# Causal attention inside a macaron block: score matmuls on 64-row tiles, and the maximum stream in two slots of two PSUM banks

## The reference

```python
q, k, v: (4, 1024, 16 heads, 16)
scores = einsum('bqhe,bkhe->bhqk', q, k) / sqrt(16)      # causal
attn = softmax(where(causal, scores, -inf), axis=-1)
out = einsum('bhqk,bkhe->bqhe', attn, v)
```

## Time and profile before

| | |
|---|---|
| three runs | 1534.96, 1540.11, 1540.85 us, median 1540.11 |
| profiled execution, its own time | 1542.46 us |
| its span, first to last instruction | 1540.8 us |
| TensorE busy, VectorE busy | 86%, 66% of the span |
| mean granted TensorE clock | 0.901 |
| softmax stage | about 502 to 1101 us |
| its maximum stream alone | 521.1 to 554.7 us |
| groups 0 to 14 with A units beside | 554.7 to 1067.8 us |

### The profile page before, as it was taken

How to read it: one execution, slowest core, us unless ns; L and a number is a source line. 1 busy time by engine, 2 the same in 40 slices (tenths; PEclk the granted TensorE clock), 3 DMA queues, 4 the chain that set the end, 5 groups by cost and what they waited for, 6 DMA issues and landing times. The chain is left out here.

```text
span 1540.8 us, 31184 instructions
## 1 busy us (share of the span) xinstructions
PE 1325.7 (86%) x8678; PEld 1003.7 (65%) x8709; DVE 1019.6 (66%) x2335; ACT 775.6 (50%) x1949; POOL 496.9 (32%) x651
## 2 busy tenths in 40 slices
PE   2628999899699499999998999999778269998998
PEld 1417999799588255555555555554465159997998
DVE  6594555499866777767675777773286755554787
ACT  2524556333244046666675666666546236564333
POOL 1554444255300201222211112212324554443454
PEclk9658999899899569999998999999896569999999
DMA  6503434122465712223322222200315114433233
GB/s 188 169 3 97 123 123 122 60 73 74 146 233 231 136 30 43 44 43 66 61 44 44 43 43 43 44 2 1 114 35 167 55 59 124 123 123 93 83 112 106
DMA packets 86509, 135.73 MB, mean 88 GB/s; under 512 B 12992, under 2 KB 66176, under 8 KB 83328
## 3 DMA queue, kind: packets, MB, share of 16 engines
q1 hardware_dynamic: 64896, 90.29, 22.1%
q0 software_dynamic: 13056, 35.67, 8.3%
q10 hardware_dynamic: 8448, 8.39, 1.6%
HBM read 81.35 MB, written 52.43 MB: 87 GB/s over the span
## 5 line engine op out<-in xcount | busy, mean ns | idle before, releaser
L1448 DVE TENSOR_REDUCE s_MX<-s_ps_a 128x1 f32<-128x512 f32 (+4 forms) x624 | 368.9, 643 | 133.8 <-PE s_ps_a L1515 132.2
L1422 ACT ACTIVATE s_PR<-s_ps_b 128x512 f32<-128x512 f32 (+3 forms) x768 | 343.7, 491 | 162.3 <-PE s_ps_b L1537 155.2
L1515 PE MATMUL s_ps_a<-s_KO,s_QO 96*128 96x512 f32 (+3 forms) x768 | 286.1, 422 | 22.7 <-DMA s_QO<-qk_scratch 22.7
L1537 PE MATMUL s_ps_b<-s_QO,s_KO 98*128 98x512 f32 (+3 forms) x768 | 266.6, 368 | 7.2 <-issue 3.9
L1391 POOL TENSOR_SCALAR_AFFINE_SELECT s_PR<-s_PR 128x256 f32<-128x256 f32 x256 | 103.5, 407 | 474.5 <-ACT s_PR L1422 473.6
L1537 PEld LDWEIGHTS s_ps_b<-s_QO,s_KO 98*128 98x128 f32 x768 | 146.3, 194 | 72.6 <-ACT s_PR L1422 54.4
L603 POOL DMA_INDIRECT f_XG<-xn_scratch,f_tok_u x144 | 136.4, 947 | 167.3 <-PE f_ps_x L700 157.4
L1515 PEld LDWEIGHTS s_ps_a<-s_KO,s_QO 96*128 96x128 f32 x768 | 152.1, 211 | 28.7 <-DVE s_MX L1448 20.8
L810 POOL DMA_INDIRECT f_YG<-y_scratch,f_slots_u x128 | 121.0, 945 | 150.2 <-DVE X L885 94.6
L1552 PE MATMUL s_ps_o<-s_PR,s_VG 128*17 128x512 f32 (+3 forms) x1536 | 163.0, 496 | 5.3 <-POOL s_PR L1391 5.3
L656 DVE TENSOR_TENSOR f_xl<-f_ps_x,f_xh 128x256 fp32r<-128x256 f32 x144 | 61.1, 425 | 97.7 <-ACT f_xh L628 92.6
(11 more groups left out here) (206 smaller groups left out, 2966.9 us busy)
## 6 DMA issues: line engine op xcount, KB each, us to landing
y_scratch<-f_YS SPq DMA_DIRECT2D x144, 128.0 KB
s_KO<-qk_scratch SPq DMA_DIRECT2D x48, 256.0 KB, 5.8
s_QO<-qk_scratch SPq DMA_DIRECT2D x96, 128.0 KB, 6.6
xn_scratch<-f_XN ACTq DMA_DIRECT2D x16, 512.0 KB, 3.2
qk_scratch<-p_QKh SPq DMA_DIRECT2D x32, 256.0 KB
qk_scratch<-p_QKl SPq DMA_DIRECT2D x32, 256.0 KB
f_stage<-in_w_up SPq DMA_DIRECT2D x20, 352.0 KB
X<-in_x SPq DMA_DIRECT2D x4, 1024.0 KB, 9.4
```

The costliest lines, as they stand in the source:

```text
L1422: nc.scalar.activation(PR[:, u // 2 % SLOTS, u % 2, 0:W - lo], ps_b[u % RING][:, lo:W], ACT.Exp, scale=SCALE).then_inc(exp_done, 1)
L1448: nc.vector.tensor_reduce(MX[:, h:h + heads, i, s], ps_a[v % RING][:, 0:heads * keys].rearrange("p (h n) -> p h n", h=heads), AX.X, ALU.ma ...
L1515: last = nc.tensor.matmul(ps_a[v % RING][:, at:at + keys], QO[k][0:R, h, i * P:(i + 1) * P], KO[k][0:R, h % 2, s * W:s * W + keys], start= ...
L1537: nc.tensor.matmul(ps_b[u % RING][:, lo:W], KO[k][0:RM, h % 2, i * P:(i + 1) * P], QO[k][0:RM, h, hf * W + lo:(hf + 1) * W], start=True, s ...
```

## The change

- **Operands.** The two heads of a pair go to rows 0 to 47 and 64 to 111 (48 rows a head: three parts of 16), the two max rows behind them at 48, 49 and 112, 113. Nothing is zero padded: QO is half as long, its memsets are gone, and VectorE sets rows 32 to 63 and 96 to 127 of every KO to one. A load is 12 DMAs of 128 KB (before: nine) with the same bytes, a `place_max` 4 DMAs of 8 KB (before: two of 16 KB).
- **Matmuls.** A and B matmuls have 48 and 50 rows and lie in rows 0 to 63 or 64 to 127 of the array. The two heads of a pair write to different banks.
- **A units.** A unit is both heads c of a pair in the two banks of a slot, up to 512 columns in each, read by one reduce of up to 1024 columns. A group has 21 units (before: 39). ps_a is two slots of two banks; ps_t is gone.
- **Masks.** With 64 rows the mask takes two matmuls (j = 0, 1) in each bank: four a diagonal unit, before one.
- **Turned tiles** use the slots of ps_a too, in one sequence with the A units (`USES`). Every use waits for the last reader of the use before the last (`slot_read`).
- **Order.** A unit counts by step are 3, 2, 1, 1, 2, 2, 2, 3, 2, 2, 1, 0 for steps 0 to 11 (in columns of VectorE 2560, 1536, 512, 1024, 1792, 1792, 2048, 2560, 1536, 2048, 1024, 0). `turn_output` and `turn_max` stand behind h = 1, ahead of the PV; on VectorE `normalise` and `max_low` stand behind the first A unit of the step and ahead of the others.

```diff
-    PH = 2 * HD
-    R = 3 * PH
+    R = 3 * HD
     RM = R + 2
+    TILE = P // 2
-            wide = W // keys
-            starts = range(0, GH, wide)
-            A_UNITS += [(i, s, h, min(wide, GH - h), keys) for h in starts]
+            wide = min(W // keys, 2)
+            A_UNITS += [(i, s, hp, wide, keys) for hp in range(0, 2, wide)]
...
+    OUT_T = MAX_T - 1
+    USES = []
+    for n in range(NB):
+        beside = [("a",) + one for one in A_BESIDE[n]]
+        USES += beside[:1]
+        if n == 1:
+            USES.append(("out", -1, 1))
+        if n == OUT_T:
+            USES.append(("out", 0, 0))
+        if n == MAX_T:
+            USES.append(("max", 1, 0))
+        USES += beside[1:]
...
-        ps_a = [ps(f"ps_a{i}", [P, W]) for i in range(RING)]
+        ps_a = [ps(f"ps_a{i}", [P, 2, W]) for i in range(2)]
-        ps_t = ps("ps_t", [P, W])
...
-            nc.vector.memset(QO[0][0:RM, :, :].bitcast(F32), 0.0).then_inc(zeros[0], 1)
-            nc.vector.memset(KO[0][R:RM, :, :].bitcast(F32), 1.0).then_inc(ones, 1)
+            for k in range(4):
+                for c in range(2):
+                    rows = slice(c * TILE + 32, (c + 1) * TILE)
+                    nc.vector.memset(KO[k][rows, :, :].bitcast(F32), 1.0).then_inc(ones, 1)
...
-                    nc.vector.tensor_reduce(MX[:, h:h + heads, i, s],
-                                            ps_a[v % RING][:, 0:heads * keys].rearrange("p (h n) -> p h n", h=heads),
-                                            AX.X, ALU.max).then_inc(a_read, 1)
+                    for c in range(2):
+                        dve.wait_ge(a_done[c], NA * g + v + 1)
+                    _, slot = slot_of_a(g, v)
+                    scores = ps_a[slot][:, :, 0:heads * keys].rearrange("p c (h n) -> p c h n", h=heads)
+                    nc.vector.tensor_reduce(MX[:, :, hp:hp + heads, i, s], scores, AX.X,
+                                            ALU.max).then_inc(slot_read, 1)
...
-                    if v >= RING or since(g, 1):
-                        pe.wait_ge(a_read, NA * g + v + 1 - RING)
+                    if not isinstance(g, int) or q >= 2:
+                        pe.wait_ge(slot_read, q - 1)
                     if diagonal:
-                        nc.tensor.matmul(scores[:, :, keys - P:keys], identb[:, :], neg[:, 0:heads, :],
-                                         start=True, stop=False, skip_group_check=True)
+                        for j in range(2):
+                            for c in range(2):
+                                rows = slice(c * TILE, (c + 1) * TILE)
+                                scores = banks[c][:, 0:heads * keys].rearrange("p (h n) -> p h n", h=heads)
+                                nc.tensor.matmul(scores[:, :, keys - P + j * TILE:keys], identb[rows, j, :],
+                                                 neg[rows, 0:heads, 0:P - j * TILE],
+                                                 start=j == 0, stop=False, skip_group_check=True)
+                    for hp in range(hp0, hp0 + heads):
+                        at = (hp - hp0) * keys
+                        for c in range(2):
+                            rows = slice(c * TILE, c * TILE + R)
+                            last = nc.tensor.matmul(banks[c][:, at:at + keys], QO[k][rows, hp, i * P:(i + 1) * P],
+                                                    KO[k][rows, hp, s * W:s * W + keys], start=not diagonal,
+                                                    stop=True, skip_group_check=True)
+                            if hp == hp0 + heads - 1:
+                                last.then_inc(a_done[c], 1)
...
-                nc.tensor.matmul(ps_b[u % RING][:, lo:W], KO[k][0:RM, h % 2, i * P:(i + 1) * P],
-                                 QO[k][0:RM, h, hf * W + lo:(hf + 1) * W], start=True, stop=True).then_inc(b_done, 1)
+                rows = slice(h % 2 * TILE, h % 2 * TILE + RM)
+                nc.tensor.matmul(ps_b[u % RING][:, lo:W], KO[k][rows, h // 2, i * P:(i + 1) * P],
+                                 QO[k][rows, h // 2, hf * W + lo:(hf + 1) * W],
+                                 start=True, stop=True).then_inc(b_done[h % 2], 1)
...
-                        if h == GH - 1:
-                            if n >= 1:
-                                pv_step(g, k, n - 1)
+                        if h == 1:
                             if n == 1 and since(g, 1):
                                 turn_output(g - 1, 1)
-                            if n == MAX_T - 1:
+                            if n == OUT_T:
                                 turn_output(g, 0)
                             if n == MAX_T and until(g, 1, NG):
                                 turn_max(g + 1)
+                        if h == GH - 1 and n >= 1:
+                            pv_step(g, k, n - 1)
```

More of the change, by code:

```diff
@@ L1258, in softmax_stage, with slot_use, slot_of_a @@
     MAX_T = 1 + max(n for n in range(NB) if (1, NA - 1) in A_BESIDE[n])
+    OUT_T = MAX_T - 1
[10 more added lines that the diff above has]
+        USES += beside[1:]
+    NU = len(USES)
+    FIRST = NA + 1 + AHEAD
+    def slot_use(g, what, ahead, index=0):
+        at = USES.index((what, ahead, index))
+        if not isinstance(g, int):
+            return FIRST - 1 + NU * g + at, (FIRST - 1 + at) % 2
+        q = FIRST + sum(0 <= n + use[1] < NG for n in range(g + 1) for use in USES[:at if n == g else NU])
+        return q, q % 2
+    def slot_of_a(g, v):
+        if isinstance(g, int) and g * NA + v < NA + AHEAD:
+            q = v + g * (NA + 1)
+            return q, q % 2
+        ahead = 1 if v >= AHEAD else 2
+        return slot_use(g - ahead, "a", ahead, v)
     SLOTS = 6
-    LOAD = 9 * 16
-    PLACE = 2 * 16
-    assert GH == 4 and D // G == 64 and GH * NB % RING == 0 and NB * 2 % SLOTS == 0 and MAX_T < NB
+    LOAD = 12 * 16
+    PLACE = 4 * 16
+    assert GH == 4 and D // G == 64 and GH * NB % RING == 0 and NB * 2 % SLOTS == 0 and MAX_T < NB and NU % 2 == 0
+    assert all(len(A_BESIDE[n]) <= GH for n in (1, OUT_T, MAX_T))
     with ExitStack() as c:
@@ L1273, in ring @@
             return [sem(f"{name}{i}") for i in range(n)]
-        QO = [sb(f"QO{i}", [P, GH, L], F32R) for i in range(4)]
+        QO = [sb(f"QO{i}", [P, 2, L], F32R) for i in range(4)]
         KO = [sb(f"KO{i}", [P, 2, L], F32R) for i in range(4)]
@@ L1315, in softmax_stage, with max_slot, out_slot @@
         recip = sem("recip")
-        att_done = sem("att_done")
         block = c.enter_context(nc.Block())
+        def max_slot(g):
+            return (NA, NA % 2) if isinstance(g, int) and g == 0 else slot_use(g - 1, "max", 1)
+        def out_slot(g, hf):
+            return slot_use(g + hf, "out", -hf, hf)
         def turn(g, k, back):
@@ L1411, in copy_output @@
                 nc.scalar.activation(OS[:, :], ps_o[:, :], ACT.Copy).then_inc(o_copied, 1)
+            act.wait_ge(consts, 4)
+            for c in range(2):
+                rows, other = slice(c * TILE, (c + 1) * TILE), slice((1 - c) * TILE, (2 - c) * TILE)
+                nc.scalar.activation(identb[rows, c, :], ident[rows, :], ACT.Copy).then_inc(halves, 1)
+                nc.scalar.activation(identb[rows, 1 - c, other], ident[rows, rows], ACT.Copy).then_inc(halves, 1)
+            nc.scalar.activation(neg[TILE:P, :, :], low[TILE:P, :, :], ACT.Copy).then_inc(halves, 1)
             max_high(0, 0)
@@ L1474, in normalise, with a_beside @@
                     turned[:, :, :, 0:HD], RC[:, :, :].unsqueeze(3).to_broadcast([P, 4, GH, HD]),
-                    ALU.mult).then_inc(att_done, 1)
+                    ALU.mult).then_inc(slot_read, 1)
+            def a_beside(g, groups, v):
+                if until(g, groups, NG):
+                    a_units(g + groups, [v])
+                    if v == NA - 1:
+                        combine(g + 1)
             a_units(0, range(NA))
@@ L1493, in _ @@
                         max_low(g + 1)
+                    for groups, v in A_BESIDE[n][1:]:
+                        a_beside(g, groups, v)
             normalise(NG - 1, 3, 1)
@@ L1507, in a_units @@
                     if diagonal:
-                        scores = ps_a[v % RING][:, 0:heads * keys].rearrange("p (h n) -> p h n", h=heads)
-                        nc.tensor.matmul(scores[:, :, keys - P:keys], identb[:, :], neg[:, 0:heads, :],
-                                         start=True, stop=False, skip_group_check=True)
-                    for h in range(h0, h0 + heads):
-                        at = (h - h0) * keys
-                        last = nc.tensor.matmul(ps_a[v % RING][:, at:at + keys], QO[k][0:R, h, i * P:(i + 1) * P],
-                                                KO[k][0:R, h % 2, s * W:s * W + keys], start=not diagonal,
-                                                stop=True, skip_group_check=True)
@@ L1518, in a_units @@
-                    last.then_inc(a_done, 1)
+                        for j in range(2):
```

(3 more changed lines are left out.)

125 lines of the change are left out of this document (57 added, 68 removed).

## The result

| | before | after |
|---|---|---|
| median of 4 runs, us | 1540.48 (1534.96 to 1543.17) | 1643.54 (1634.16 to 1648.76) |
| ratio, 95% interval | | 1.0667 (1.061 to 1.0724) |
| profiled execution, span, us | 1540.8 | 1642.8 |
| mean granted clock | 0.901 | 0.814 |
| first B unit of group 0, us | 554.72 | 560.72 |

Slower by 6.7%, where the forecast said 2.3% and its range ended at 1630. The span grew by 102.0 us: 6.0 up to the first B unit, 89.4 in groups 0 to 14, 7.2 in group 15; the rest of the program was 0.6 shorter.

What follows compares the result with a forecast made beforehand. TensorE's stream of matmuls was taken to set the pace in the softmax groups. From 1542.5 us, +22 (slots and order), +18 (clock) and -4 (start) gave 1578.5, or 1576 against the median of 1540.1; range 1515 to 1630.

Steps and rivals of the forecast that it cites:

- The clock: Groups 0 to 14: one fall to 0.50 a group, as in group 15, 1.2 us each; +18 us.
- the gain of the tiles: A units, and where two B units meet: row tiles side by side save some 5 us a group and perhaps 1.5.
- Slots and order: Groups 0 to 14: TensorE held up by two slots and the new order; +1.5 us a group, +22 us.
- The walk's steps: One group from first B unit to first B unit, by steps: 6.9, 11.4, 9.2, 3.5, 4.2; sum 35.2 us against 33.73.
- Start: Before the groups: shorter memsets and maximum stream, DMA issues at nothing, first place_max under 1 us; together -4 us.
- The three more DMA issues of each load: Operand loads at the start: more DMAs, same bytes; put at nothing (ends -1 and +2 us).
- The maximum stream alone: Ahead of the groups: 24,576 columns in place of 25,088, 27.1 us against 29.4; -2.3 us.
- The -1.7 of the memsets: VectorE's first two memsets ahead of the first load: 3.5 us in place of 5.2.
- Slots that keep up: Faster rival: slot refills come in time, a group takes 28 to 30 us, the whole 1465 us; chance 0.22.
- Clock holds: Rival: slot waits stay but the clock doesn't fall; 1558 us, or 1536 with the walk too long; chance 0.30.
- Serial row tiles: Slower rival: A pairs run one after another, +4 us a group on top, 1636 us; chance 0.10.
- the sum of TensorE's waits for VectorE: Sign in the profile: rises from the mask loads' 30 us to 80 and more, mostly in steps 1, 7, 8 and 9.

Runs made afterwards that it cites:

- e3: The changed kernel with every B matmul issued twice, 768 more matmuls; 1624.2 us, ratio 1.0547 to the kernel before.
- e5: The kernel before with score matmuls cut to half rows (A to the first 64, B to the other 34), scores incomplete; 1605.3 us, ratio 1.0424.
- r1: The kernel before, with its ring of three banks, ps_t and order, on 64-row tiles in 42 A units; 1633.1 us, ratio 1.0624.
- e2: The changed kernel with the loads of groups 2 and 3 put behind the first place_max; 1634.6 us, ratio 1.0637 to the kernel before.
- e7: The changed kernel with each load's 12 DMAs reordered, so neighbours in the queue go to different groups of 16 partitions; 1636.9 us, one run.
- e6: The kernel before without the query loads, so queries are zeros, all rows kept; 1534.4 us, ratio 0.9955.
- e4: The changed kernel with projection rows reordered, so each partition's piece of a load is one run of 8 KB; 1639.3 us, ratio 1.0674.

## Why the prediction was right and wrong

**The sum of what happened.** The price of half clock comes from single groups of one schedule, against 33.96 at full clock: 1.03 for 3.5 us, 4.0 for 12.1, 6.4 for 20.2; 0.3 us each. So 301 us in groups 0 to 14 cost 90, the 18 before cost 5: 85 of the 89.4. The other 4 can't be split with certainty. A group at full clock is 0.2 to 0.3 longer for waits, which gives 3 to 5. And where the hardware loop goes from group 7 to group 8, TensorE stops once for 3.9 us before the change and twice after it, for 3.97 and for 4.02:

```profile
881.80 0.79 PE L1570 MATMUL s_ps_a<-s_KO,s_QO 48*128 48x512 f32 x2 [4.02 <-issue]
```

The price of half clock, 0.29 to 0.33 by the three groups, is uncertain by as much. In group 15, 26 us against 7 cost 6 of the 7.2. With the 6.0 of the start that is 101 of 102.0.

**The sign was right, by the two mechanisms that the forecast named; their sizes were not.**

*The clock was mis-sized: +18 in the forecast, some +91 measured.* The step that failed is the length of a fall in "they look like group 15 ... A fall costs at most half of 3.4 us ... I take one a group (ends none and three)". The count was near, 13 falls in fifteen groups, and so nearly was the price of a microsecond of half clock (1.2 for 3.4 us, measured 0.3 each). But I took every fall to be as short as the two of group 15. Only two of the 13 were; with the late rise at the start, half clock came to 20 us a group in place of 3.4. Why it stays low so long is known in part. e3 shows that fewer columns one after another are part of it: more of them, on the same rows, brought half clock from 332 to 87 us. e5 and r1 show that going over to row halves is what lets the clock down. In e5 it stays at 1.2 GHz while TensorE is busy for 84.6 of 86 us, so idle time is not needed for it. Whether the rows as such weigh in, or only that matmuls side by side leave fewer columns one behind the other, no run separates. In the changed kernel pairs side by side cut TensorE's busy time from 33.4 to 28.9 us a group at full clock. So what I had booked as the gain of the tiles is most likely itself the cause of the loss. The rule of the Trainium skill weighed in the prediction (TensorE: Matmul & The Clock Gate, section Why this matters for your kernels), by which only idle time between bursts brings the clock down, would have given 18 us less than the forecast and 91 less than the result. The traces overrule it here: in the changed kernel TensorE stands idle for 4 us twice, at the loop's turn, and otherwise never for 1 us between 562 and 1163 us, and yet the clock fell 13 times.

*Slots and order: +22 in the forecast, +4 measured.* The walk's steps stand against 33.96: 0 and 1 6.75 without the fall (forecast 6.9), 2 to 6 11.06 (11.4), 7 4.99 (5.3), 8 3.68 (3.9), 9 3.24 (3.5), 10 and 11 4.22 (4.2). Against before each cut moved the way that the walk said; but all except the last were 0.15 to 0.35 us too long, 1.2 in all: I added latencies where they partly overlap. (My own terms for steps 0 and 1, 4.95, 0.4, 0.5, 0.26 and 0.99, add up to 7.1 and not to 6.9.) The exchange the prediction named is there, but smaller on both sides: I had the tiles save some 5 us a group and slots and order take them back; r1 with the old ring saves 0.9 (32.80), and slots and order give back 1.2 (33.96). Most of what the tiles take off TensorE goes to waits already in r1.

*Start: -4 in the forecast, +6 measured.* "The three more DMA issues of each load ... the bytes are the same, and I put them at nothing (ends -1 and +2)" and "the first (under 1 us)" of `place_max` failed. The maximum stream alone was as forecast: 31.3 us in e2, where nothing waits, against 33.6, so -2.3. The -1.7 of the memsets did not arrive: from the first memset to the first A unit it takes 19.5 us in place of 17.8, since the loads run at 119 GB/s in place of 173. And four loads were queued ahead of the max rows, and TensorE waited 8.18 us for the small DMAs behind them. I priced issues and bytes, and not the rate, nor the queue. Counted from the first memset the start is 7.8 us longer; the stage itself began 1.8 earlier in the profiled run.

*Rivals.* Slots that keep up: fell, as TensorE's masks wait 0.9 us for VectorE in step 7 (585.98) and again in step 8 (590.55), over the 0.3 named; step 1's last A unit waits only 0.17 (at 1098.30), but the turned output ahead of it 0.73. And a group at full clock is 34, not 28. Clock holds: fell by the first look at the clock line. Serial row tiles: fell, with A pairs at 0.48 us and r1's 2.8 us less of TensorE. Its time (1636) came near by luck, by another cause, which is why the rows of a pair were the thing to look at and not the total. Of the signs I named for the forecast, the sum of TensorE's waits for VectorE (80 and more) came to 74.3, if all its weight loads are counted. But the larger waits are those of the B units for ScalarE, 9.0 us of e2's group at full clock against 2.5 before, and the walk had named that wait for steps 2 to 6 only.

**What stays open.** Whether the granted clock weighs the rows of a matmul at all, or only the columns that enter one behind the other, is not settled: e5, r1 and the changed kernel alter both. A run that would settle it has half rows with A and B in the same row half, so that nothing runs side by side. The rest of the slower loads (e7 recovers 13 of 54 GB/s) and the second stop at the loop's turn weren't explained.

## What to carry to other kernels

Before tiling a TensorE-bound stage by rows, put a price on the clock: a stage at 99% busy on whole rows ran at 1.00, the same stage on row halves, with matmuls side by side, fell to 0.50 for long stretches, and in the changed kernel the clock cost some 91 us where the waits at full clock cost some 4. Price it as half-clock time in a stage, not in single falls, and remove matmul time only where the stage's end moves with it. Small DMAs that a stage's start waits for go ahead of bulk loads that nobody needs yet: here 8.4 us for a move of three lines.

## What the runs showed of the hardware that I had not expected

- TensorE's busy time does not tell its clock: e5, on row halves side by side, 0.50 at 39.5 of 40 us busy; e6, on whole rows one after another and with zeros for data, 1.00 at 39.6 of 40; the maximum stream of the kernel before, on whole rows, 0.50 at 10.0 of 10.
- Issuing 768 matmuls more made the kernel faster (1643.5 to 1624.2 us), by the clock.
- Alternating 64-row and whole-height matmuls costs 78.6 us a group against 53.0 at the same clock, and 42% of the kernel.
- The run-to-run scatter grew with the clock's share: four runs of the kernel before lie within 0.5%, those of the 64-row versions within 0.6 to 2.4%. The time of the changed kernel follows the clock of each run, from 1634.2 us at 0.825 to 1648.8 at 0.809.
- Eight-kilobyte packets gave no more than four-kilobyte ones (e4, 118 GB/s, against 119), so packet size told nothing.
- At the turn of the hardware loop TensorE stopped for 3.9 us with nothing to wait for that the trace shows; in the changed kernel, twice for 4.0.
